# An attention and mixture-of-experts layer: eight groups of 256 queries in place of six mixed ones, maxima ahead of the low part, prefix product two steps earlier

## What is computed

```
xn  = layernorm(x)
q, k, v = split(xn @ w_qkv.T)                    # 128 wide each
att = softmax(q @ k.T / sqrt(8)) @ v @ w_proj.T + b_proj     # one head over all 2048 keys
h   = xn @ W_in + b_in
top-2 of 8 experts by h @ W_gate + b_gate, weights from a softmax over the two
moe = sum over the two of  weight * (relu(h @ W1[e] + b1[e]) @ W2[e] + b2[e])    # 128 -> 512 -> 128
out = x + att + moe @ W_out + b_out
```

## Time and profile before

| | us |
|---|---|
| median of 3 runs | 266.45 (265.16 to 271.34) |
| the profiled execution | 266.31 |
| its span, first to last instruction | 264.5 |
| mean granted TensorE clock | 0.974 of full speed |
| TensorE matmuls busy | 233.3 |
| VectorE busy | 147.9 |
| ScalarE busy | 119.0 |
| GpSimd busy | 142.2 |

### The profile page before, as it was taken

The page is one execution under the profiler, slowest core; times in us unless marked ns, Lnnn a source line. Parts: engine busy times, 40 slices in busy tenths (PEclk is TensorE's granted clock), DMA queues, the critical chain, the costliest instruction groups (busy, mean ns, idle before and its releaser), DMA issues.

```text
span 264.5 us, 4573 instructions
## 1 busy us (share of the span) xinstructions
PE 233.3 (88%) x1590; PEld 211.6 (80%) x1590; DVE 147.9 (56%) x340; ACT 119.0 (45%) x275; POOL 142.2 (54%) x163
## 2 busy tenths in 40 slices
PE   8898695978898888979999999999999489888994
PEld 8797594766686666779999999999988278788993
DVE  5945756277517867353545454545576535785462
ACT  1644240240264444733454545454477426546461
POOL 4029005888888810014666665656068888888300
PEclk9999898999999999999999999999999959999999
DMA  6799700111111021001222222222111113112011
GB/s 198 310 309 332 196 2 30 41 40 42 40 40 41 30 72 30 0 10 32 74 68 74 68 72 72 71 71 61 36 36 42 46 45 71 40 42 69 22 40 41
DMA packets 23047, 19.53 MB, mean 74 GB/s; under 512 B 3280, under 2 KB 19696, under 8 KB 22768
## 3 DMA queue, kind: packets, MB, share of 16 engines
q1 hardware_dynamic: 20000, 14.71, 18.5%
q0 software_dynamic: 2048, 4.20, 5.8%
q10 hardware_dynamic: 976, 0.33, 0.5%
HBM read 10.97 MB, written 8.26 MB: 73 GB/s over the span
## 4 chain that ended last, share of the span: by engine, by line
PE 67%; DVE 12%; POOL 6%; ACT 5%; issue 5%; DMA 3%; ACTq 1%; POOLq 0%; DVEq 0%
PE ps L1037 13%; PE ps L1023 13%; DVE part_max L598 7%; PE ps L848 5%; POOL wtab L380 5%; PE ps L789 4%; PE ps L791 4%; PE ps L790 4%; PE ps L910 3%; PE ps L797 3%; PE ps L923 3%; PE ps L919 3%; PE ps L920 3%; DMA w_raw<-in_L_attn_w_proj_dram 2%; ACT pf L455 2%
## 5 line engine op out<-in xcount | busy, mean ns | idle before, releaser
L343 POOL COPY wst<-wtab 128x1156 f32 x39 | 45.0, 1153 | 51.3 <-DVE y_sb L735 51.2
L608 DVE TENSOR_TENSOR pl<-pf,ph 128x512 fp32r<-128x512 f32 x48 | 35.2, 733 | 34.4 <-ACT pf L455 33.4
L455 ACT ACTIVATE pf<-ps 128x512 f32<-128x512 f32 x64 | 38.0, 594 | 28.9 <-PE ps L791 21.7
L454 ACT ACTIVATE ph<-ps 128x512 fp32r<-128x512 f32 x48 | 28.7, 599 | 38.6 <-PE ps L791 35.7
L598 DVE TENSOR_REDUCE part_max<-ps 128x1 f32<-128x1024 f32 x32 | 38.8, 1219 | 10.9 <-PE ps L848 8.6
L353 POOL DMA_INDIRECT slots_in<-hl,slots x32 | 32.8, 1024 | 21.8 <-DVE slots L674 14.8
L1037 PE MATMUL ps<-wst,mid 128*128 128x128 f32 x312 | 41.3, 275 | 0.9 <-DVE x_sb L625 0.9
L380 POOL DMA_INDIRECT wtab<-slots_out,slots x32 | 33.0, 1031 | 16.1 <-DMA slots_out<-y_sb 8.4
L1023 PE MATMUL ps<-xgT,wst 128*128 128x128 f32 x312 | 41.3, 275 | 0.0
L727 DVE TENSOR_SCALAR mid<-ps,wst 128x128 f32<-128x128 f32 x78 | 23.7, 346 | 28.9 <-PE ps L1023 28.9
L1037 PEld LDWEIGHTS ps<-wst,mid 128*128 128x128 f32 x312 | 38.0, 192 | 1.1 <-issue 1.0
(11 more groups left out here) (145 smaller groups left out, 359.0 us busy)
## 6 DMA issues: line engine op xcount, KB each, us to landing
wtab<-in_L_ffn_W_dram SPq DMA_DIRECT2D x16, 256.0 KB, 6.2
xg<-slots_in SPq DMA_DIRECT2D x39, 64.0 KB, 2.0
slots_out<-y_sb SPq DMA_DIRECT2D x39, 64.0 KB, 1.5
slots_in<-wst SPq DMA_DIRECT2D x2, 1024.0 KB, 5.0
x_sb<-in_L_attn_x_dram SPq DMA_DIRECT2D x4, 256.0 KB, 4.9
out_dram<-x_sb SPq DMA_DIRECT2D x3, 256.0 KB
wtab<-in_L_ffn_b_dram SPq DMA_DIRECT2D x1, 512.0 KB, 7.4
slots_in<-hl,slots POOLq DMA_INDIRECT x32
```

What stands on the lines that cost most here:

```text
L343: pool.tensor_copy(wst[:, t % 4, :], wtab[:, bass.ds(experts[t], 1), :].rearrange("p a n -> p (a n)")).then_inc(Z["staged"], 1)
L455: act.activation(pf[:, i % 3, :], ps[:, st_bank(i), :], ACT.Exp).then_inc(Z["pf_done"], 1)
L608: dve.tensor_tensor(pl[:, i % 3, :], pf[:, i % 3, :], raw(ph[:, i % 3, :]), ALU.subtract).then_inc(Z["lo_done"], 1)
```

## The change

It does four things.

1. All groups have 256 queries. There are eight, four ahead of the experts and four behind. The steps remain 32 and 32. A step that had three score matmuls of 512 columns has six of 256, and its three value matmuls of 512 become six of 256. `PAIR_STEP` now has four pairs in each group but the last, at steps 4, 5, 5 and 6 of the first and at 1, 2, 4 and 5 of the others. Ahead of the experts stand 20 pairs (24 before), behind them 12 (8 before).
2. VectorE takes the maxima of a step ahead of that step's `low`, where it took `low` first.
3. On TensorE a step's second pair (there is one only in the first group's step 5) stands behind that step's `values`. `prefix` moves from step 3 of the first group to step 1.
4. The three blocks move from steps 12, 21 and 25 to 14, 22 and 26. The waits between blocks and pairs, which share banks, are computed from the tables: a block waits for the maxima of the pairs issued so far, a pair for the blocks issued in earlier steps.

```diff
-    GROUPS = [(0, 256), (256, 256), (512, 512), (1024, 512), (1536, 256), (1792, 256)]
-    PRE = 3
+    GROUPS = [(256 * g, 256) for g in range(8)]
+    PRE = 4
-    PAIR_STEP = [[4, 5, 5, 6], [1, 2, 2, 3, 3, 4, 4, 5], [1, 2, 4, 5, 7, 8, 10, 11], [1, 4, 7, 10], [1, 2, 3, 4], []]
+    PAIR_STEP = [[4, 5, 5, 6]] + 6 * [[1, 2, 4, 5]] + [[]]
-    BLOCK_AT = {12: 0, 21: 1, 25: 2}
+    BLOCK_AT = {14: 0, 22: 1, 26: 2}
@@ VectorE, ahead of the experts; behind them alike
-                    if FIRST[g] + k >= PLAIN:
-                        low(FIRST[g] + k)
                     for m in pairs_at(g, k):
                         pair_max(g + 1, m)
                     if k == PAIR_STEP[g][-1]:
                         row_max(g + 1)
+                    if FIRST[g] + k >= PLAIN:
+                        low(FIRST[g] + k)
@@ TensorE, beside
-                for m in pairs_at(g, k):
-                    if m == 0:
-                        pe.wait_ge(Z["q_hi_ready"], g + 2)
-                    if g > PRE:
-                        pe.wait_ge(Z["moe_added"], 1)
-                    pair(g + 1, m)
+                for m in pairs_at(g, k)[:1]:
+                    step_pair(g, k, m)
+
+            def step_pair(g, k, m):
+                if m == 0:
+                    pe.wait_ge(Z["q_hi_ready"], g + 2)
+                blocks = sum(at < FIRST[g] + k - BASE_B for at in BLOCK_AT)
+                if g >= PRE and blocks > 0:
+                    pe.wait_ge(Z["moe_added"], blocks)
+                pair(g + 1, m)
@@ TensorE, steps ahead of the experts
-                    if g == 0 and k == 3:
+                    if g == 0 and k == 1:
                         prefix()
                     beside(g, k)
                     if i >= 2:
                         values(i - 2)
+                    for m in pairs_at(g, k)[1:]:
+                        step_pair(g, k, m)
@@ TensorE, blocks
-            def moe_transpose(b):
+            def moe_transpose(b, pairs):
                 pe.wait_ge(Z["c_ready"], TB * (b + 1))
-                if b == 0:
-                    pe.wait_ge(Z["max_read"], FIRST_PAIR[PRE + 2])
-                else:
-                    pe.wait_ge(Z["max_read"], FIRST_PAIR[NG])
+                pe.wait_ge(Z["max_read"], pairs)
...
-                        moe_transpose(BLOCK_AT[s])
+                        moe_transpose(BLOCK_AT[s], FIRST_PAIR[g + 1] + sum(at <= k for at in PAIR_STEP[g]))
```

More of the change, by code:

```diff
@@ L765, in _ @@
                     s = i - BASE_B
-                    low(i)
                     for m in pairs_at(g, k):
@@ L770, in _ @@
                         row_max(g + 1)
+                    low(i)
                     if k == 0 and g + 1 < NG:
@@ L1101, in _ @@
             values(LAST - 1)
-            moe_transpose(NR - 1)
+            moe_transpose(NR - 1, FIRST_PAIR[NG])
             for r in range(ROUNDS[NG - 1]):
```

## The result

The changed kernel takes 248.16 us (median of 4 runs, 247.24 to 248.57), and the ratio to the kernel before is 0.932, with an interval of 0.9275 to 0.9369. The two profiled executions, 266.31 and 248.09, are 18.2 us apart. Some executions of a kernel fall into a second, slower state, more than 1.5% above its fastest, and the medians, ranges, differences and ratios given from here on leave them out. The forecast was 246.3, in a range of 242.0 to 252.5. The profiled execution of the changed kernel took 248.09 us, with a span of 246.3.

What follows compares the result with a forecast made beforehand. TensorE's queue, idle mostly at pairs waiting for VectorE's maxima and at the first block behind the experts, bounds it. 30.8 + 66.7 + 75.2 + 65.3 + 6.5 = 244.5 span, plus 1.8: 246.3 us, range 242.0 to 252.5.

Steps and rivals of the forecast that it cites:

- the signs named: Signs if right: pair waits under 5 us (13.9 before), no first-block wait above 1, clock near 1 behind the experts.
- Prices: On TensorE, from start to start: a step of 512 queries 1.38 us, a step of 256 1.44, a pair 0.47.
- The rival of bare weight loads: On TensorE, in steps of 256: short matmuls lay weight loads bare, making the kernel slower, 273 us; chance 0.03.
- First group: TensorE, 30.8 to 51.6 us: earlier routing and a fuller clock save 1.7 each, 3.4 in all, to 17.4.
- Second group: TensorE, 51.6 to 75.1 us: four pairs leave (1.9), waits go (4.8), other work shrinks by 0.5: 16.3.
- Third and fourth group: TensorE, in place of 75.1 to 111.3 us: two groups of 16.0 each, plus 1.0 for collisions: 33.0.
- collisions: On VectorE, differences held up by GpSimd's weight copies ahead of the experts: 1.0 us added, 5.7 by the full rule.
- Late scatters: Ahead of layer 1: scatters' path 96.6, TensorE's 97.5; as rival, layer 1 at 99.0, total 250.3 us, chance 0.08.
- Experts: Stretch of 77.4 us: one round of small stages less and shorter waits take 2.2 off, to 75.2.
- Behind the experts: From 188.7 us on, 69.3 before: TensorE's work 60.7 plus waits, first block's wait and slow clock gone: 65.3.
- the side-by-side walk: TensorE's and VectorE's queues behind the experts: waits of 0.7 (step 2), 0.4 (10), 0.5 (11), 3.4 us in all.
- The rival in which gathers hold VectorE: Behind the experts: sums hold the differences and maxima queued behind them, no gain there, 250.3 us; chance 0.14.

Runs made afterwards that it cites:

- experiment 6: Changed kernel with the prefix product back at step 3 of the first group: 248.95 us, ratio 0.937.
- Experiment 10: Changed kernel with the group sizes, the number of groups ahead of the experts and the pair table of the kernel before: 253.33 us, ratio 0.954.
- Experiment 4: Changed kernel with groups of 256, 256 and 512 ahead of the experts, the 512 group's pairs at steps 1, 4, 7, 10: 250.87 us, ratio 0.944.

## Why the prediction was right

**The sum.** The span is 1.8 us above the forecast. By the table, the terms that came out longer are the start (0.4), the first group (1.2) and the third and fourth (1.5); the others came out 0.2 to 0.4 shorter each, 1.3 together. Of the signs named, those on waits and on the clock came true. The places came later: the first prefix product at 34.61 for 34.1, the first tile load at 93.64 for 92.5, and layer 1 of tile 0 at 100.17, outside its 96.5 to 98.5.

**What bounds.** That TensorE's queue with its waits at VectorE decides, and not the busy share of any engine, held: VectorE's busy time even rose (147.9 to 149.5 us), while the span fell by 18.2.

**Prices.** Ninety-six more score matmuls and as many value matmuls cost what the rows said. A whole step of 256 took 1.44 us in the changed kernel again, here in TensorE's timeline near the end of the attention:

```profile
234.19 0.28 PE L789 MATMUL ps<-q_hi,xnT_hi 128*128 128x256 f32 x1
...
235.63 0.28 PE L789 MATMUL ps<-q_hi,xnT_hi 128*128 128x256 f32 x1
```

The rival of bare weight loads is excluded; weight loads were busy 60.2 of 65.1 us behind the experts, beside the matmuls.

**First group, 17.4 forecast, 18.6 measured.** Routing did come earlier: slots at 39.58 for 40.86, 1.3 and not 2.2 earlier, since the group started 0.4 later and TensorE ran at the lower clock up to 36.6 in this execution, where it was up to 33.7 before. I had priced the clock behind the waits (which stayed at 1.00) and taken the one at the start as given. The first pair's maximum no longer waited for routing. Of the three pairs that I had waiting 0.8 each, the first did not wait, and the others waited 0.45 and 0.60; the row of maxima waited 0.65, as it had before.

**Second group, 16.3 and 15.9.** No wait is left, as the prediction had it from 1.91 against 1.84. From pair to pair it took 2.03 here (52.64 to 54.67), a little more room still.

**Third and fourth group, 33.0 and 34.5.** This is the term that was missed by most, and not for its waits. The prediction allowed 2.4 us for them and 1.0 for collisions. TensorE stood idle for 1.7 in all: 0.81 at a pair and 0.85 at `project`. What was too small is the count of TensorE's own work, 2 x 14.8 = 29.6 us, where its matmuls were busy for 32.8. The stretch ends at layer 1, and ahead of layer 1 stand the `values` of the last two steps, with two transposes:

```profile
98.43 0.27 PE L1018 MATMUL ps<-ident,xg 128*128 128x128 f32 x1
98.46 0.36 PE L919 MATMUL ps<-ph,xn_hi 128*128 128x256 f32 x1
...
99.31 0.30 PE L1018 MATMUL ps<-ident,xg 128*128 128x128 f32 x1
99.37 0.36 PE L919 MATMUL ps<-ph,xn_hi 128*128 128x256 f32 x1
```

With layer 1 at 100.17 these are 1.7 us. The prediction counted them (as 1.4) on the path of the scatters and not on TensorE's. The other 1.5 is spread over the steps: one whose pair follows close on another took 2.07, with 1.91 counted:

```profile
76.13 0.28 PE L789 MATMUL ps<-q_hi,xnT_hi 128*128 128x256 f32 x1
...
76.91 0.74 PE L848 MATMUL ps<-xnT_hi,q_hi 128*128 128x512 f32 x2
...
78.20 0.28 PE L789 MATMUL ps<-q_hi,xnT_hi 128*128 128x256 f32 x1
```

Both waits stand behind a collision. The two differences ahead of them took 1.81 and 1.67 us, both beside a copy of weights on GpSimd. VectorE's and GpSimd's rows:

```profile
83.34 1.81 DVE L608 TENSOR_TENSOR pl<-pf,ph 128x512 fp32r<-128x512 f32 x1 [0.75 <-ACT pf L455]
...
88.57 1.67 DVE L608 TENSOR_TENSOR pl<-pf,ph 128x512 fp32r<-128x512 f32 x1
```

```profile
83.42 1.17 POOL L343 COPY wst<-wtab 128x1156 f32 x1
...
88.53 1.16 POOL L343 COPY wst<-wtab 128x1156 f32 x1
```

The difference and the copy start within 0.1 us of each other, and the difference ends about 0.6 after the copy, nearly its own 0.69. That is the whole-instruction exclusion that the Trainium skill states (SBUF — State Buffer, "Who interferes with whom"), and the rows agree with it. There was such a row before too, 2.16 us. VectorE has next to no slack in a pair step now, so that being 1.0 to 1.1 us late there is TensorE's wait.

**Late scatters.** The two paths were forecast to nearly tie, 96.6 and 97.5. They came to about 97.8 (tile 0 at 96, and the 1.7 from its transpose to layer 1) and 100.2. Scatters did not decide in any run; experiment 6 settles it.

**Experts, 75.2 and 74.8,** as forecast. Experiment 10 has 77.4 there with groups of 512 and all else changed, so the gain there comes from the group size.

**Behind the experts, 65.3 and 65.1.** That the total agrees so well is in part luck. TensorE's own work was counted as 60.7 and its matmuls were busy for 63.1 (in which waits too short to show may be hidden); the waits were put at 4.6 and its idle time was 2.1. Work that was missed and waits that did not come cancelled. The mechanism held: the block's wait and the low clock behind it went, and the three largest new waits of the side-by-side walk stood at the steps named. What the prediction did not say, and experiment 10 shows, is that this part owes its gain to VectorE's order and the blocks' places: with the groups of before it takes 63.2 of the 69.3, and the smaller groups add the 1.9 of their four more pairs. The rival in which gathers hold VectorE is excluded for the time, but part of it is real: the waits of 0.34 and 0.89 stand behind sums that VectorE waited for.

**Overlooked.** The second pair behind `values` was priced at nothing in the prediction. In the changed kernel it can act in one step only, as no other has two pairs. Experiment 4 shows what it is worth where there are more: 1.7 us less of waiting in a group with three such steps.

## What to carry to other kernels

When a producer waits for a single place to be free, look at what the consumer has queued ahead of the read that frees it: taking the read first, and the work that is wanted only two steps later second, was worth 6.6 us for exchanging two lines. Read the cadence of such a pair from the trace (here 1.9 to 2.0 us a pair step against 0.62 + 1.22 for the pair and its maximum) before spreading or packing work; where the two nearly tie, any instruction that falls between them becomes a wait. Smaller groups help at the borders between phases, where whole groups are emptied one stage after the other, and hardly within a phase: in experiment 4 a group of 512 with its pairs spread, in place of two of 256, cost 0.5 us ahead of the experts and 2.7 in them. And when a forecast cuts a queue into stretches, count what lags across the cut: here the `values` run two steps behind, and the last 1.7 us of them stood in no term of TensorE's sum.

## What the runs showed of the hardware that was not expected

- The clock at the first scores differs between programs and executions with the same wait of 1.6 us ahead of them. The mean granted clock from 31 to 34 us was 0.51 before, 0.50 after and 0.50 to 0.63 in the variants without dummies, but 1.00 in the run with only the prefix product moved; from 34 to 37 us it was 0.56 after and 0.58 when the same kernel ran again, but 0.98 with the prefix product at step 3. With seven dummy matmuls in the wait it was 1.00 from 28 to 37 us in all three profiles.
- A low clock that hides behind another wait is cheap: taking it away in the first group brought 0.8 to 1.3 us and not 2.7, since 25 matmuls sooner meant 1.0 us more of waiting for routing.
- A difference of 128x512 took 1.67 to 1.81 us beside a weight copy of 1.17 us that began within 0.1 us of it, and 0.68 to 0.69 in most other places.
